# Causal softmax attention on one core: transposes of the weights three tiles behind the scores instead of two

## The chip, the cores and the metric

One of the cores of a Trainium2 chip runs the whole program. The metric is the device time in microseconds (us) of one execution. The core's engines used here are TensorE (PE, with PEld for its weight loads), VectorE (DVE), ScalarE (ACT), GpSimd (POOL) and the queue of SyncE (SP), which issues the DMAs. Each engine works through its own instructions in order; they wait for each other by semaphores.

## The reference

The program is a transformer-like chain with residual additions: attention A, a feed-forward layer, attention B (hyperbolic distances), and the feed-forward layer again. The change lies in attention A alone, with 2 batches of 2048 tokens, 16 heads of width 64:

```
x = x + attn_a(layernorm(x));  x = x + ffn(layernorm(x));  x = x + attn_b(layernorm(x));  x = x + ffn(layernorm(x))
attn_a:
    q, k, v = x @ Wq, x @ Wk, x @ Wv                      # 16 heads of 64
    scores = q @ k.T * 64**-0.5 + slope[h] * (i - j)      # masked where j > i
    out = softmax(scores) @ v                             # all heads side by side
    return out @ Wo + bo
```

All data are float32.

## The kernel before

Attention A works through 2 batches, and in each through 8 pairs of heads. A loop over the batches holds a loop of 7 turns over the first seven pairs, and after it the eighth pair written out once more. So of the 16 pairs 12 are followed by a taken branch back to the start of the loop's body, 2 by the branch that isn't taken, and 2 end a batch. Before the pairs of a batch all four engines make the normalized and transposed input `xnT` and the projections q and k of the first pair.

A query tile is 128 rows. The 16 tiles of a pair are taken from the longest (tile 15, all 2048 key columns) to the shortest (tile 0, 128 columns, since the mask is causal). The work on the n-th of them is:

- **S(n)**, "scores": TensorE multiplies q by k for both heads at once into PSUM, in slots of up to 512 columns (4 slots for n = 0 to 3, then 3, 2 and 1). VectorE adds the position bias, writes the row to `srow` in SBUF and takes the row's maximum in the same instruction (L598), one for each head and slot. Two slots have PSUM banks, so that TensorE is at most two slots ahead of VectorE (L758). L604 makes the negated maximum of the tile.
- **exponential** (ScalarE, L674): one for each head over the whole row, in place, with the sum. ScalarE issues both for tile n-1 at the start of step n, ahead of its copies of that step.
- **invert** (VectorE, L579 and L582): reciprocal of the sum and multiplication of the row, for tile n-1 in step n, one head in the middle of the step and one at its end.
- **T**, "transposes": TensorE transposes the weights out of `srow` in groups of four blocks of 128 x 128, each head to itself, into a ring of three PSUM banks (L773). The first group of a tile waits for `scaled`, that is for L582 (L770). ScalarE and VectorE copy each bank to `pT` (L523 and L661). A fixed table, `on_dve`, says which of the two engines does it, and each entry waits until the entry three before it has been copied (L490).
- **A(k)**, "product with v": for two tiles at once, once both are transposed (L791). **C(k)**: ScalarE copies the result to `oT`. **O(k)**: TensorE multiplies by Wo (L802) and VectorE adds to X (L615).
- **V**: four groups of projections of v (L743), in steps 0 and 1. **P**: the eight projections of q and k for the next pair (L730), in the last four steps, two in each. VectorE copies k, ScalarE copies q.

The order is written by `order(n)`: for each step n a list of these items, which every engine follows for its own part. In a step S, A and T are interleaved slot by slot. Before the change T of tile n-2 stands in step n, A and C in the even steps from 4, O in the odd ones from 5, and a pair has 20 steps. A row of `srow` may be overwritten once the tile that held it has been transposed (L593). After the last step VectorE branches back to the next pair's first step at L651, TensorE at L836 and ScalarE at L711.

Of the kernel before, what the change touches and what calls it, by code (L numbers as in the profile page):

```python
# [20 lines left out]
TB = SEQ // P  # L21
# [357 lines left out]
def stage_attn_a(nc, env, wqk, wv, wo, bo, slopes):  # L379
# [11 lines left out]
    parts = [[(a, min(a + 4, 2 * ib + 2)) for a in range(0, 2 * ib + 2, 4)] for ib in reversed(range(NIB))]  # L391
    part0 = [sum(len(c) for c in parts[:k]) for k in range(NIB + 1)]
    NPA = part0[NIB]
    ROWS = 3
    LAG = 2
    STEPS = TB + 4
    PROJ = ["q3", "k0", "k1", "k2", "k3", "q2", "q1", "q0"]
    NPR = len(PROJ)

    def order(n):  # L400

        m, k = n - LAG, (n - 4) // 2
        s = [("S", i) for i in range(len(slots[n]))] if n < TB else []
        t = [("T", i) for i in range(len(groups[m]))] if 0 <= m < TB else []
        a = [("A", i) for i in range(len(parts[k]))] if n >= 4 and n % 2 == 0 else []
        seq = []
        for i in range(max(len(s), len(t), len(a), 1)):
            seq += s[i:i + 1]  # L410
            if i == 0 and n >= 5 and n % 2:
                seq += [("O", k)]
            seq += a[i:i + 1] + t[i:i + 1]
            if n < 2 and i % 2:
                seq += [("V", 2 * n + i // 2)]
        if a:
            seq += [("C", k)]
        if n >= TB:
            seq += [("P", 2 * (n - TB)), ("P", 2 * (n - TB) + 1)]
        return seq  # L420


    ring = []
    for n in range(STEPS):
        for what, i in order(n):
            ring += {"T": [("T", n - LAG, i, 0), ("T", n - LAG, i, 1)], "V": [("V", i)], "O": [("O", i)]}.get(what, [])
    NEV = len(ring)
# [4 lines left out]
    def count(upto):  # L432
        return sum(on_dve[:upto])
# [4 lines left out]
    with ExitStack() as ctx:  # L438
        def sb(n, shape, dt=F32):
            return ctx.enter_context(nc.sbuf_tensor(f"a_{n}", shape, dt))  # L440
# [14 lines left out]
        v_sb = sb("v", [P, TB, 2 * DH])  # L455
        srow = sb("srow", [P, ROWS, 2, SEQ])
        xn = srow[:, 0, 0, 0:4 * D].rearrange("p (j d) -> p j d", d=D)
# [21 lines left out]
        def bank(i, a=0, b=BANK):  # L479
            return env.psum[:, i * BANK + a:i * BANK + b]  # L480

        def rows(h):
            return slice(h * DH, (h + 1) * DH)
# [25 lines left out]
        def copy_weights(eng, copy, g, n, i, dve_side):  # L509
            a, z = groups[n][i]  # L510
            il = tiles[n] % 2
            for h in range(2):
                e = place["T", n, i, h]
                if on_dve[e] != dve_side:
                    continue
                eng.wait_ge(bank_done, g * NEV + e + 1)

                if n >= 2:
                    k = n // 2 - 1
                    eng.wait_ge(av_done, g * NPA + (part0[k] + i + 1 if n % 2 == 0 else part0[k + 1]))  # L520
                else:
                    eng.wait_ge(av_done, g * NPA)
                copy(pT[:, h, a:z, il * P:(il + 1) * P],  # L523
                     bank(T_BANKS[e % 3], 0, (z - a) * P).rearrange("p (j i) -> p j i", i=P)
                     ).then_inc(dve_evac if dve_side else act_evac, 1)
# [37 lines left out]
        def _(dve):  # L563
# [9 lines left out]
            def body(b, hp, last):  # L573
# [3 lines left out]
                def invert(m, h):  # L577
                    dve.wait_ge(exp_done, (g * TB + m) * 2 + h + 1)
                    nc.vector.reciprocal(zinv[:, m, h:h + 1], zsum[:, m, h:h + 1]).then_inc(zinv_done, 1)  # L579
                    dve.wait_ge(zinv_done, (g * TB + m) * 2 + h + 1)  # L580
                    row = srow[:, m % ROWS, h, 0:(tiles[m] + 1) * P]
                    nc.vector.tensor_scalar(row, row, zinv[:, m, h:h + 1], None, ALU.mult).then_inc(scaled, 1)  # L582

                for n in range(STEPS):
                    m = n - 1
                    seq = order(n)
                    for j, (what, i) in enumerate(seq):
                        if what == "S":
                            a, z = slots[n][i]
                            c = slot0[n] + i  # L590
                            if i == 0:

                                dve.wait_ge(bank_done, g * NEV + (tile_end[n - ROWS] if n >= ROWS else 0))  # L593
                            off = SEQ - P - tiles[n] * P
                            for h in range(2):
                                dve.wait_ge(scores_done, (g * NSL + c) * 2 + h + 1)
                                dve.sem_inc(passed, 1)
                                nc.vector.tensor_tensor_reduce(  # L598
                                    out=srow[:, n % ROWS, h, a:z], in0=bank(c % 2 * 2 + h, 0, z - a),
                                    in1=bias[:, h, off + a:off + z], scale=1.0, scalar=-3e38, op0=ALU.add, op1=ALU.max,  # L600
# [7 lines left out]
                        if what == "T":  # L608
                            copy_weights(dve, nc.vector.tensor_copy, g, n - LAG, i, True)
                        if what == "O":  # L610
# [46 lines left out]
        def _(act):  # L657
# [12 lines left out]
            def exponential(g, n, h):  # L670
                width = (tiles[n] + 1) * P
                act.wait_ge(nmax_done, g * TB + n + 1)
                row = srow[:, n % ROWS, h, 0:width]
                nc.scalar.activation(row, row, ACT.Exp, bias=nmax[:, n, h:h + 1],  # L674
                                     accum_out=zsum[:, n, h:h + 1]).then_inc(exp_done, 1)

            def body(b, hp, last):
                g = b * PAIRS + hp
                for n in range(STEPS):
                    m = n - 1  # L680
# [3 lines left out]
                    for j, (what, i) in enumerate(seq):  # L684
# [4 lines left out]
                        if what == "T":  # L689
                            copy_weights(act, copy, g, n - LAG, i, False)  # L690
                        if what == "C":
# [24 lines left out]
        def _(pe):  # L716
# [17 lines left out]
            def values(g, i):  # L734

                if i == 0:
                    pe.wait_ge(wv_loaded, (g + 1) * 16)
                e = place["V", i]
                bank_free(pe, g, e)
                ps = bank(T_BANKS[e % 3])  # L740
                for t in range(4):
                    for c in range(KC):
                        last = nc.tensor.matmul(ps[:, t * P:(t + 1) * P], xnT[:, c, (4 * i + t) * P:(4 * i + t + 1) * P],  # L743
                                                wv_sb[:, c, :], start=(c == 0), stop=(c == KC - 1))
                last.then_inc(bank_done, 1)

            def scores(g, n, i):
                a, z = slots[n][i]
                c = slot0[n] + i
                if c == 0:  # L750

                    pe.wait_ge(k_copied, (g + 1) * 4)
                    pe.wait_ge(q_copied, g * 4 + 2)
                if c == 1:
                    pe.wait_ge(q_copied, (g + 1) * 4)
                if c >= 2:

                    pe.wait_ge(max_done, (g * NSL + c - 1) * 2)  # L758
                pe.sem_inc(passed, 1)
                for h in range(2):  # L760
                    nc.tensor.matmul(bank(c % 2 * 2 + h, 0, z - a), q_sb[rows(h), tiles[n] * P:(tiles[n] + 1) * P],  # L761
                                     k_sb[rows(h), a:z], start=True, stop=True, skip_group_check=True
                                     ).then_inc(scores_done, 1)

            def transposes(g, n, i):
                a, z = groups[n][i]
                for h in range(2):
# [4 lines left out]
                    for jt in range(a, z):  # L772
                        last = nc.tensor.transpose(bank(T_BANKS[e % 3], (jt - a) * P, (jt - a + 1) * P),  # L773
                                                   srow[:, n % ROWS, h, jt * P:(jt + 1) * P], env.ident[:, :])
                    last.then_inc(bank_done, 1)

            def product_with_v(g, k, i):


                ib = NIB - 1 - k  # L780
                if i == 0:

                    e = tile_end[2 * k + 1]
                    pe.wait_ge(dve_evac, g * n_dve + count(e))
                    pe.wait_ge(act_evac, g * n_act + e - count(e))
                    pe.wait_ge(oT_done, g * NIB + k)
                    pe.sem_inc(passed, 1)
                for jt in range(*parts[k][i]):
                    lo = P if jt == 2 * ib + 1 else 0
                    for h in range(2):  # L790
                        last = nc.tensor.matmul(bank(6, lo, IB)[rows(h), :], v_sb[:, jt, rows(h)], pT[:, h, jt, lo:IB],  # L791
                                                start=(jt == 0), stop=(jt == 2 * ib + 1), skip_group_check=True)
                last.then_inc(av_done, 1)
# [12 lines left out]
            def body(b, hp, last):  # L806
                g = b * PAIRS + hp
                for n in range(STEPS):
                    for what, i in order(n):
                        if what == "S":  # L810
                            scores(g, n, i)
                        if what == "V":
                            values(g, i)
                        if what == "T":
                            transposes(g, n - LAG, i)
                        if what == "A":
                            product_with_v(g, (n - 4) // 2, i)
                        if what == "O":
                            out_projection(g, i)
                        if what == "P" and not last:  # L820
                            project(g + 1, i)
# [808 lines left out]
```

## Time and profile before

| | before |
|---|---|
| median of 3 runs | 6132.58 us (6128.41 to 6133.12) |
| profiled execution, its own time | 6132.41 us |
| span of the profiled execution | 6130.6 us |
| attention A in it | from about 48 to 2339 us |
| one head pair inside the loop | 141.3 us (632.24 to 773.54 us) |
| PE busy | 4058.3 us (66% of the span) |
| DVE busy | 4679.5 us (76%) |
| ACT busy | 4508.2 us (74%) |
| POOL busy | 1421.4 us (23%) |

The span is the time from the first to the last instruction in the record of one execution. A busy time is the union of the instructions' durations on an engine, over all stages together. The stages have different limits, so that these shares don't say what bounds attention A; the rows of a pair do. In a timeline a row merges neighbouring instructions of one form, and a bracket at its end gives how long the engine had been idle before it and which instruction ended that wait.

### The profile page before, as it was taken

What the parts mean: (1) busy time and instruction counts of PE and PEld (TensorE: products, weight loads), DVE (VectorE), ACT (ScalarE), POOL (GpSimd) and SP (SyncE); (2) the same over time, 40 slices, a digit from 0 to 9 for tenths busy, and PEclk for the clock granted to TensorE, in tenths of its full rate; (3) what the DMA queues carried; (4) which work ended last, traced back from release to release, by engine and by line L of the source; (5) the groups of instructions that cost most, each with busy time, mean ns of one, the idle gap of its engine ahead of it and who ended that gap; (6) DMA issues with size and microseconds to landing.
All of it is one profiled execution on the core that took longest, in us unless ns stands there. A gap on an engine that the chain in (4) does not pass through costs nothing. (4 is left out here: it accounts for less than half of the span.)

```text
span 6130.6 us, 71245 instructions
## 1 busy us (share of the span) xinstructions
PE 4058.3 (66%) x22020; PEld 1846.5 (30%) x22020; DVE 4679.5 (76%) x7176; ACT 4508.2 (74%) x3663; POOL 1421.4 (23%) x1211
## 2 busy tenths in 40 slices
PE   6999999899999997444444444445355444444446
PEld 4555555555555555210101110102111111110104
DVE  6666666666666665699889898884889898989865
ACT  3555555455555553289999999996499999999992
POOL 0000000000000000144444444430244444445320
PEclk9999999999999997667767777777566677777767
DMA  1000000000000000288888888884488888888871
GB/s 35 5 5 5 5 8 5 5 6 5 5 5 5 5 2 3 77 173 184 182 186 182 185 185 181 186 172 120 123 186 183 180 187 180 188 174 185 181 153 58
DMA packets 137220, 628.82 MB, mean 103 GB/s; under 512 B 28038, under 2 KB 66120, under 8 KB 66632
## 3 DMA queue, kind: packets, MB, share of 16 engines
q0 software_dynamic: 73728, 536.90, 43.7%
q1 hardware_dynamic: 63048, 86.55, 4.1%
q8 instruction: 211, 3.46, 0.2%
q14 instruction: 233, 1.91, 0.1%
HBM read 65.30 MB, written 21.23 MB: 14 GB/s over the span
## 5 line engine op out<-in xcount | busy, mean ns | idle before, releaser
L1272 DVE SCALAR_TENSOR_TENSOR b_tiles<-b_ra_rep,b_cap,psum 128x1024 f32<-128x1024 f32 x1024 | 1260.7, 1270 | 246.9 <-PE psum L1503 234.7
L598 DVE CUSTOM_DVE_ANT_0 a_srow<-psum,a_bias 128x512 f32<-128x512 f32 (+3 forms) x1280 | 727.5, 607 | 518.0 <-PE psum L761 488.9
L1503 PE MATMUL psum<-b_qT,b_kT 126*128 126x512 bf16 x2048 | 763.4, 484 | 500.3 <-DVE b_tiles L1272 497.4
L661 ACT ACTIVATE a_pT<-psum 128x512 f32<-128x512 f32 (+3 forms) x1056 | 511.4, 527 | 656.1 <-PE psum L773 656.1
L1516 PE MATMUL psum<-b_tiles,b_v_aug 128*32 128x512 f32 x2464 | 449.3, 814 | 682.1 <-ACT b_tiles L1416 682.0
L1279 DVE TENSOR_SCALAR b_tiles<-b_tiles 128x2048 f32<-128x2048 f32 x512 | 665.6, 1300 | 5.5
L773 PE MATMUL psum<-ident,a_srow 128*128 128x128 f32 x4352 | 624.9, 280 | 67.7 <-DVE a_pT L523 31.1
L761 PE MATMUL psum<-a_k,a_q 64*128 64x512 f32 (+3 forms) x2560 | 626.8, 573 | 7.2 <-DVE a_cmax L598 6.1
L674 ACT ACTIVATE a_srow<-a_srow,a_nmax 128x1536 f32<-128x1536 f32 (+15 forms) x512 | 610.3, 1197 | 21.7 <-DVE a_nmax L604 19.6
L1416 ACT ACTIVATE b_tiles<-b_tiles,b_sc 128x4096 f32<-128x4096 f32 x154 | 585.5, 3802 | 5.1
L1516 PE MATMUL psum<-X,b_v_aug 128*32 128x512 f32 x1632 | 294.7, 806 | 442.2 <-ACT X L1416 442.2
L1403 ACT ACTIVATE b_tiles<-b_tiles 128x4096 f32<-128x4096 f32 x154 | 552.7, 3612 | 26.2 <-DVE b_tiles L980 25.3
L773 PEld LDWEIGHTS psum<-ident,a_srow 128*128 128x128 f32 x4352 | 474.8, 140 | 317.7 <-issue 146.4
L199 POOL MEMSET ffn_rank<- 128x1 f32 x16 | 0.7, 99 | 2413.4 <-POOLq L74 2413.4
L1410 ACT ACTIVATE b_tiles<-b_tiles 128x4096 f32<-128x4096 f32 x154 | 555.8, 3609 | 0.9
L791 PE MATMUL psum<-a_pT,a_v 128*64 128x256 f32 (+1 forms) x4608 | 540.6, 374 | 15.1 <-ACT a_pT L661 11.6
L980 DVE TENSOR_TENSOR b_tiles<-b_tiles 128x2048 f32<-128x2048 f32 x232 | 535.8, 2310 | 0.6
L1503 PEld LDWEIGHTS psum<-b_qT,b_kT 126*128 126x128 bf16 x2048 | 156.8, 108 | 1237.3 <-DVE b_tiles L1272 945.3
L980 POOL TENSOR_TENSOR b_tiles<-b_tiles 128x2048 f32<-128x2048 f32 x76 | 273.4, 3597 | 651.9 <-PE psum L1516 643.4
L582 DVE TENSOR_SCALAR a_srow<-a_srow,a_zinv 128x1536 f32<-128x1536 f32 (+15 forms) x512 | 402.8, 787 | 18.2
L791 PEld LDWEIGHTS psum<-a_pT,a_v 128*64 128x64 f32 x4608 | 312.2, 136 | 283.5 <-issue 171.8
L1403 ACT ACTIVATE X<-X 128x4096 f32<-128x4096 f32 x102 | 366.7, 3612 | 39.1 <-DVE X L980 38.5
(209 smaller groups left out, 5887.2 us busy)
## 6 DMA issues: line engine op xcount, KB each, us to landing
b_tiles<-b_tiles POOLq DMA_DIRECT2D x308, 1024.0 KB, 12.7
X<-b_tiles POOLq DMA_DIRECT2D x204, 1024.0 KB, 12.9
b_ra_rep<-ra_scratch SPq DMA_DIRECT2D x32, 1024.0 KB, 6.8
x_scratch<-X SPq DMA_DIRECT2D x8, 1024.0 KB, 10.6
kv_scratch<-b_tiles SPq DMA_DIRECT2D x4, 2048.0 KB, 8.6
X<-x_scratch SPq DMA_DIRECT2D x8, 1024.0 KB, 10.7
X<-in_x_dram SPq DMA_DIRECT2D x4, 1024.0 KB, 9.4
a_wqk<-in_wqk_dram SPq DMA_DIRECT2D x32, 128.0 KB, 2.6
```

Of the source, the lines that this page charges most:

```text
L598: nc.vector.tensor_tensor_reduce(out=srow[:, n % ROWS, h, a:z], in0=bank(c % 2 * 2 + h, 0, z - a), in1=bias[:, h, off + a:off + z], scale= ...
L674: nc.scalar.activation(row, row, ACT.Exp, bias=nmax[:, n, h:h + 1], accum_out=zsum[:, n, h:h + 1]).then_inc(exp_done, 1)
L761: nc.tensor.matmul(bank(c % 2 * 2 + h, 0, z - a), q_sb[rows(h), tiles[n] * P:(tiles[n] + 1) * P], k_sb[rows(h), a:z], start=True, stop=Tru ...
L773: last = nc.tensor.transpose(bank(T_BANKS[e % 3], (jt - a) * P, (jt - a + 1) * P), srow[:, n % ROWS, h, jt * P:(jt + 1) * P], env.ident[:, :])
L791: last = nc.tensor.matmul(bank(6, lo, IB)[rows(h), :], v_sb[:, jt, rows(h)], pT[:, h, jt, lo:IB], start=(jt == 0), stop=(jt == 2 * ib + 1) ...
L980: engine.tensor_tensor(y_slot(h, k), a, a, ALU.mult).then_inc(S["sq_" + name], 1)
L1272: nc.vector.scalar_tensor_tensor(out=a[:, s * HALF:(s + 1) * HALF], in0=ra_rep[:, j, s * HALF:(s + 1) * HALF], scalar=cap[:, j, k:k + 1], ...
L1279: nc.vector.tensor_scalar(a, a, 1.0, 1.0 + GUARD, ALU.add, ALU.max).then_inc(S["a_ready"], 1)
L1403: nc.scalar.activation(y, y, ACT.Sqrt, bias=-1.0).then_inc(S["root_done"], 1)
L1416: nc.scalar.activation(y, y, ACT.Exp, bias=col(SHIFT), scale=col(NEG_S)).then_inc(S["w_done"], 1)
L1503: last = nc.tensor.matmul(half_ps(s)[:, i * BANK:(i + 1) * BANK], kT[:, j, k * P:(k + 1) * P], qT[:, j, cs], start=True, stop=True)
L1516: last = nc.tensor.matmul(bank(4 + j)[32 * i:32 * i + 32, :], v_aug[:, j, k, :], y_slot(h, k)[:, i * BANK:(i + 1) * BANK], start=(k == 0), ...
```

## The change

The transposes of a tile come three steps after its scores instead of two. Since a row then stays in use one step longer, `srow` gets four rows instead of three. Everything behind the transposes is one step later too: A and C stand in the odd steps from 5 to 19, O in the even ones from 6 to 20, and a pair has 21 steps. The projections for the next pair stay in steps 16 to 19, so that the last step holds O(7) alone. The order of the entries in the ring of PSUM banks, and which engine copies each, is the same as before, entry for entry.

```diff
-    ROWS = 3
-    LAG = 2
-    STEPS = TB + 4
+    ROWS = 4
+    LAG = 3
+    STEPS = TB + LAG + 2
...
-        m, k = n - LAG, (n - 4) // 2
+        m, k = n - LAG, (n - LAG - 2) // 2
         s = [("S", i) for i in range(len(slots[n]))] if n < TB else []
         t = [("T", i) for i in range(len(groups[m]))] if 0 <= m < TB else []
-        a = [("A", i) for i in range(len(parts[k]))] if n >= 4 and n % 2 == 0 else []
+        a = [("A", i) for i in range(len(parts[k]))] if n >= LAG + 2 and (n - LAG) % 2 == 0 else []
...
-            if i == 0 and n >= 5 and n % 2:
+            if i == 0 and n >= LAG + 3 and (n - LAG) % 2:
                 seq += [("O", k)]
...
-        if n >= TB:
+        if TB <= n < TB + 4:
             seq += [("P", 2 * (n - TB)), ("P", 2 * (n - TB) + 1)]
...
                         if what == "A":
-                            product_with_v(g, (n - 4) // 2, i)
+                            product_with_v(g, (n - LAG - 2) // 2, i)
```

TensorE, at the end of a pair inside the loop. L730 are projections for the next pair, L802 is O(7), L798 and L488 its waits for the copy of the result and for a free bank, and L836 is the branch back. The rows with a minus are of before, those with a plus of the change:

```order
-L798 REGISTER_ALU
-L488 REGISTER_ALU
-L802 MATMUL psum<-a_wo,a_oT 128x256 x2
 L728 REGISTER_ALU
 L730 MATMUL psum<-a_xnT,a_wqk 128x512 x2
 L728 REGISTER_ALU
 L730 MATMUL psum<-a_xnT,a_wqk 128x512 x2
+L798 REGISTER_ALU
+L488 REGISTER_ALU
+L802 MATMUL psum<-a_wo,a_oT 128x256 x2
 L836 REGISTER_ALU
 L836 COMPARE_AND_BRANCH
```

O(7) has moved from ahead of the last two projections, P6 and P7, to behind them, and is now the last thing that TensorE does in a pair.

TensorE, from the end of step 1 of a pair into step 2, before. L743 is the last group of v, L758 the wait for a free pair of score banks, L770 and L490 the waits of the transposes L773:

```order
L743 MATMUL psum<-a_wv,a_xnT 128x128 x8
L758 ISA
L761 MATMUL psum<-a_k,a_q 128x512 x2
L770 ISA
L490 REGISTER_ALU
L773 MATMUL psum<-ident,a_srow 128x128 x4
L770 REGISTER_ALU
```

The same engine with the change, from the third slot of step 2 to the first transposes, which now stand in step 3:

```order
L758 ISA
L761 MATMUL psum<-a_k,a_q 128x512 x2
L758 ISA
L761 MATMUL psum<-a_k,a_q 128x256 x2
L758 ISA
L761 MATMUL psum<-a_k,a_q 128x512 x2
L770 ISA
L490 REGISTER_ALU
L773 MATMUL psum<-ident,a_srow 128x128 x4
```

The four slots of step 2 now follow each other on TensorE with nothing between them, and the transposes of the first tile begin behind the first slot of step 3.

## Rows read from the trace of the kernel before

**Rows 1.** Windows inside one pair: step 2, step 3, and the pair's sum

```profile
648.57:657.89 9.32, 8.26 (x49) 4.59 (x48) 7.98 (x22) 7.33 (x11) 0.00 (x0) 1.00 0.05 15
657.89:666.23 8.34, 7.69 (x47) 4.39 (x46) 7.41 (x21) 6.65 (x11) 0.00 (x0) 1.00 0.01 3
...
sum 141.30, PE 135.36 PEld 80.26 DVE 93.46 ACT 76.93 POOL 0.00; mean PE 33.84 PEld 20.07 DVE 23.37 ACT 19.23 POOL 0.00
```

Their columns: from and to, length, then busy time and instructions of PE, PEld, DVE, ACT and POOL, granted clock, DMA share and GB/s; the sum has the busy times alone.

**Rows 2.** Groups by line of PE, over the same pair: busy, mean, idle before

```profile
L773 PE MATMUL psum<-ident,a_srow 128*128 128x128 f32 x272 | 39.1, 280 | 4.3 <-DVE a_pT L523 1.9 <-ACT a_pT L661 1.1 <-DVE a_srow L582 0.9
```

**Rows 3.** Timeline of PE at the loop's turn: start, length, instruction

```profile
627.85 1.03 PE L802 MATMUL psum<-a_wo,a_oT 128*128 128x256 f32 x4
628.72 3.60 PE L730 MATMUL psum<-a_xnT,a_wqk 128*128 128x512 f32 x8
632.24 1.99 PE L761 MATMUL psum<-a_k,a_q 64*128 64x512 f32 x8
634.16 2.05 PE L743 MATMUL psum<-a_wv,a_xnT 128*128 128x128 f32 x16
636.73 0.70 PE L761 MATMUL psum<-a_k,a_q 64*128 64x512 f32 x2 [0.51 <-DVE a_cmax L598]
```

**Rows 4.** Timeline of DVE at the same turn

```profile
629.03 0.69 DVE L615 TENSOR_TENSOR X<-psum,X 128x512 f32 x1 [2.00 <-PE psum L802]
635.27 0.69 DVE L598 CUSTOM_DVE_ANT_0 a_srow<-psum,a_bias 128x512 f32<-128x512 f32 x1 [5.55 <-PE psum L761]
```

**Rows 5.** Timeline of DVE where the branch isn't taken, after the seventh pair

```profile
1052.76 0.69 DVE L615 TENSOR_TENSOR X<-psum,X 128x512 f32 x1 [2.00 <-PE psum L802]
1057.30 0.69 DVE L598 CUSTOM_DVE_ANT_0 a_srow<-psum,a_bias 128x512 f32<-128x512 f32 x1 [3.84 <-PE psum L761]
```

**Rows 6.** Line L836, the branch of TensorE: least, median and greatest duration in ns

```profile
L836 PEldq COMPARE_BRANCH  x14: 83/3749/5093, 201.5 to 2201.7; - x14
```

**Rows 7.** Timeline of DVE in steps 2 and 3 of the pair

```profile
650.00 0.68 DVE L598 CUSTOM_DVE_ANT_0 a_srow<-psum,a_bias 128x512 f32<-128x512 f32 x1
...
650.61 0.69 DVE L598 CUSTOM_DVE_ANT_0 a_srow<-psum,a_bias 128x512 f32<-128x512 f32 x1
...
653.53 1.22 DVE L582 TENSOR_SCALAR a_srow<-a_srow,a_zinv 128x1920 f32<-128x1920 f32 x1
...
657.12 0.42 DVE L598 CUSTOM_DVE_ANT_0 a_srow<-psum,a_bias 128x256 f32<-128x256 f32 x1 [0.35 <-PE psum L761]
```

**Rows 8.** Timeline of ACT in steps 2 and 3 of the pair

```profile
651.05 1.89 ACT L674 ACTIVATE a_srow<-a_srow,a_nmax 128x1920 f32<-128x1920 f32 x1
...
652.93 1.07 ACT L661 ACTIVATE a_pT<-psum 128x512 f32<-128x512 f32 x2
...
658.13 1.79 ACT L674 ACTIVATE a_srow<-a_srow,a_nmax 128x1792 f32<-128x1792 f32 x1
```

**Rows 9.** Timeline of PE in steps 2 and 3 of the pair

```profile
653.57 0.66 PE L773 MATMUL psum<-ident,a_srow 128*128 128x128 f32 x4 [1.06 <-ACT a_pT L661]
...
660.26 0.65 PE L773 MATMUL psum<-ident,a_srow 128*128 128x128 f32 x4 [0.65 <-DVE a_srow L582]
```

**Rows 10.** Timeline of PE in steps 9 to 17 of the pair before

```profile
581.57 0.33 PE L773 MATMUL psum<-ident,a_srow 128*128 128x128 f32 x1 [1.06 <-DVE a_pT L523]
...
608.87 0.87 PE L791 MATMUL psum<-a_pT,a_v 128*64 128x256 f32 x8
...
610.31 1.13 PE L802 MATMUL psum<-a_wo,a_oT 128*128 128x256 f32 x4
...
612.82 1.74 PE L791 MATMUL psum<-a_pT,a_v 128*64 128x256 f32 x16 [0.72 <-ACT a_pT L661]
...
619.83 0.33 PE L773 MATMUL psum<-ident,a_srow 128*128 128x128 f32 x1 [0.28 <-DVE a_srow L582]
```

**Rows 11.** Timeline of PE between the batches

```profile
1190.38 1.97 PE L829 MATMUL psum<-ident,a_srow 128*128 128x128 f32 x8 [4.91 <-DVE a_srow L635]
```

**Rows 12.** A window behind it, with the columns of rows 1

```profile
1204.00:1209.60 5.60, 5.52 (x7) 2.43 (x8) 0.66 (x1) 0.60 (x1) 0.00 (x0) 0.50 0.00 0
```

## The prediction

> **What bounds the kernel now.** I read three things, each to answer one question. First, what limits attention A? The windows over one pair of heads inside the loop [rows 1] show TensorE busy for 135.4 of 141.3 us at full clock, VectorE for 93.5 and ScalarE for 76.9. So attention A is TensorE's work, one piece after another, plus 5.9 us a pair in which it stands still. The change gives TensorE no work more and none less: only those 5.9 us can shrink or grow, in 16 pairs. Second, what makes TensorE stand still? The group of the transposes [rows 2] has 4.3 us of it, and only 0.9 of them end with L582, the scaled row. The other 3.0 end with a copy that frees a bank of the ring, and the change leaves the ring as it is. Third, where does TensorE have little beside the scores? In steps 2 and 3 it still stands still for 1.06 and 0.65 us [rows 1], with VectorE busy for 8.0 and 7.4 us, and at the loop's turn, where the other engines start again. There I followed the timelines.
>
> **The turn of the loop.** O(7) ends on TensorE at 628.88 (627.85 + 1.03). While VectorE adds its result and branches back, TensorE has P6 and P7 (3.6 us), then slots 0 and 1 of the next pair (1.9) and the first group of v (2.05), and stands still only 0.51 us before slot 2 at 636.73 [rows 3]. Slot 2 needs VectorE to have read slot 0. VectorE adds at 629.03 and reads slot 0 only at 635.27, 6.24 us later [rows 4]. Those scores were not what it waited for: slot 0 starts at 632.24. After the seventh pair, where the branch isn't taken, the same distance is 4.54 us and ends about as the scores get there [rows 5]. The taken branch therefore keeps VectorE away until some 6.2 us after the add begins. Slot 2 starts 636.73 - 628.88 = 7.85 us after O(7)'s end whatever TensorE does in between. The Trainium skill states this ("Runtime: NRT & Kernel Launch", the section on instruction fetch mechanics): a taken branch to a page outside the current window has to wait for a DMA fetch of that page. It gives no time for it, and the sum uses none.
>
> With the change O(7) is behind P6 and P7. It still has the two projections between itself and A(7), so that its own wait stays covered, and VectorE's branch still begins only after O(7). What is left to TensorE in the 7.85 us is slots 0 and 1 and one group of v: 634.16 - 632.24 + 2.05 = 3.97 us. It stands still for 3.88 instead of 0.51: **+3.37 us, 12 times = +40**. TensorE's own branch lies in it as well. Its record lasts up to 5.1 us and 3.7 in the middle [rows 6]; before, it ran under the queued projections, and now it can begin only once O(7) is released, about 0.6 us after A(7)'s end (the copy to `oT`), with 4.5 us of work still queued. That may delay slot 0 by about a us, but slot 2 waits for VectorE anyway. At the four pair ends without a taken branch nothing is added.
>
> **The start of a pair.** Step 2 loses its transposes, 32 of 0.144 us (39.1 / 272 [rows 2]) = 4.6 us, and keeps four slots. Then VectorE sets the rate, since TensorE is at most two slots ahead. VectorE begins slot 0 of step 2 at 650.00, one head each 0.61 us, and an inversion 1.22 with some 0.15 ahead of it for the reciprocal [rows 7]. With nothing else in the way: slot 0 until 651.2, slot 1 until 652.45, first inversion until 653.8, slot 2 until 655.05, slot 3 (256 columns, 0.35 a head) until 655.75, maximum at 656.0, second inversion until 657.4. TensorE has slots 0 and 1 done by 650.7, starts slot 2 at 651.4 (0.7 idle), slot 3 behind it until 653.2, and waits until 655.2 for slot 2's maximum, before slot 0 of step 3 (2.0 idle). That is 2.8 us in the step.
>
> Step 3 then has T(0). Its first banks are copied by ScalarE behind both exponentials of tile 2. Before, in step 2, the second of them ran from 651.05 and the copies followed at 652.93 [rows 8], and TensorE waited 1.06 us for it [rows 9]. Now the exponentials start at the maximum, 656.05, take 2 x 1.79, and the first copy is done at 660.3. TensorE wants the bank at 659.0: slot 0 from 655.2, four transposes twice, slot 1, and one head's group. Idle 1.35 us. The same pattern in step 4 leaves about 0.3. Against that, the 1.06 of step 2 and the 0.65 of step 3, which ended with the scaled row [rows 9], are gone. 2.8 + 1.35 + 0.3 - 1.06 - 0.65 = **+2.74 us a pair, x 16 = +44**. A bound from below is 0, if the pattern of step 3 only moves; from above some 4, if step 4 has a wait like step 3's.
>
> **What is gained later.** The wait of 1.06 us for a copy on VectorE in step 9 [rows 10], and one like it of 0.86 in step 13, come because that copy stands behind S of the same step and one inversion. S and the inversion are one tile shorter there with the change, so that the copy comes about 0.6 and 0.3 us earlier. **-0.9 x 16 = -14.** In the last steps A(6) waited 0.72 us for the copies of T(13); P0 and P1 now stand between them. The last transposes waited 0.28 us for the scaled row, and are now a step behind it. O(5), though, has lost the slot of S(15) that stood between it and A(5): A(5) ended at 609.74 (608.87 + 0.87) and O(5) started at 610.31 behind that slot. TensorE now waits those 0.57 us, where it waited 0.14 before. -0.72 - 0.28 + 0.43 = -0.57, in the 14 pairs that have P: **-8**. VectorE's and ScalarE's own load is the same, and SP's loads wait for the same events; nothing of the other stages moves.
>
> **Sum:** 40 + 44 - 14 - 8 = +62 on the profiled execution's 6132.4, which is 0.2 below the median: **6194 us**, +1.0%. Faster or slower by 0.2% (12 us) is about what a measurement tells from no change.
>
> **The rivals.**
>
> *Faster.* The lag was the trouble, and everything TensorE waits for in a pair after its first two steps goes: the 4.3 us at the transposes [rows 2] and the 0.72 before A(6), x 16 = -80, while the start costs nothing because VectorE's backlog in step 2 is made up in step 3; the turn keeps its +40. That gives 6092. It decides in step 2: it needs VectorE to read four slots while TensorE loses less than 1 us there. Against it are the 8.0 us of VectorE in that step beside 3.9 of TensorE's, and that three quarters of the waits aren't for the scaled row. With a part of this, and no cost at the start, the time is within 12 us of before. Chances 0.07 and 0.06.
>
> *The turn costs nothing.* If VectorE's absence at the turn begins with something other than O(7), its restart would come earlier as well. Then +22 is left: 6154. That the 6.24 us follow the add in all 12 turns speaks against it. 0.08.
>
> *The clock falls at the turn.* Between the batches TensorE stands still for 4.91 us [rows 11], and in the window behind it the granted clock is 0.5, 1.2 GHz, and still is in the first 5.6 us of dense projections [rows 12]. Gaps up to 1.1 us inside a pair left it at 2.4 GHz. The new gap of 3.9 us lies between. A fall could cost half of 5.6 us of dense work, 2.8, at each of 12 turns: +34, 6228. If TensorE's branch delays slot 0, the gap is in two parts, of 1 and 2.9 us, which speaks against it. The Trainium skill ("TensorE: Matmul & The Clock Gate") has a rule of thumb that idle gaps over about 3 us bring the slow level back; it would put this rival first, and the time at 6228. No gap of 3.9 us is in the trace. 0.14.
>
> *Forecast,* waits at start and turn at full clock: 0.65, with a range of its own from 6167 to 6214 (start from 0 to 4 us, less what the later steps give, the turn from 3 to 4).
>
> **Numbers.** From 6148 to 6230 holds the forecast, the costless turn and most of the clock rival. Slower 0.87, within 0.2% 0.06, faster 0.07.
>
> **What would show it.** In the changed profile TensorE's gap before slot 2 of a pair (released by VectorE's L598) should be 3 to 4 us in 12 pairs and near 0 in those after an untaken branch; a pair in the loop should last about 145.5 to 146 us and a pair before an untaken branch about 3.4 less. In step 2 TensorE should wait twice for L598, 0.7 and 2.0 us, where L598 had almost no waiters; the wait for L582 should be gone, and the wait for ScalarE's copy should be in step 3. A granted clock below 1.0 inside a batch would show the clock rival. I'd be wrong if VectorE's restart doesn't follow O(7), or if TensorE makes up in the middle of a pair what it lost at its start; since it has no slack there, it can't by these rows.

## The result and the profile after

The changed kernel takes 6229.57 us (median of 4 runs, 6224.62 to 6231.33) against 6132.85 before (4 runs): 1.6% slower, ratio 1.0158 (1.014 to 1.0176). That is inside the range, but only 0.4 us under its top. The forecast of the likeliest case was 6194, 36 us less. The number is near the 6228 of the rival in which the clock falls too, but only in part for that rival's reasons. The profiled execution took 6224.62 us with a span of 6222.7, 92.1 more than before.

TensorE's busy time on the page rose from 4058.3 to 4081.5 us with the same number of instructions, and the granted clock has new dips inside attention A. The rest is idle time. The groups of TensorE over attention A show what it waited for (count, busy and mean, idle before it and what ended it). Two of them before, and then the changed kernel's:

```profile
L761 PE MATMUL psum<-a_k,a_q 64*128 64x512 f32 (+3 forms) x2560 | 626.8, 573 | 7.2 <-DVE a_cmax L598 6.1
L743 PE MATMUL psum<-a_wv,a_xnT 128*128 128x128 f32 x1024 | 131.3, 281 | 0.0
```

```profile
L761 PE MATMUL psum<-a_k,a_q 64*128 64x512 f32 (+3 forms) x2560 | 640.9, 587 | 88.3 <-DVE a_cmax L598 71.8 <-issue 14.1
L773 PE MATMUL psum<-ident,a_srow 128*128 128x128 f32 x4352 | 623.2, 282 | 52.2 <-DVE a_pT L523 26.2 <-ACT a_pT L661 12.9 <-DVE X L615 10.2
L791 PE MATMUL psum<-a_pT,a_v 128*64 128x256 f32 (+1 forms) x4608 | 540.6, 374 | 5.6 <-DVE a_pT L523 2.1 <-ACT a_pT L661 1.5 <-issue 0.2
L802 PE MATMUL psum<-a_wo,a_oT 128*128 128x256 f32 x512 | 142.5, 401 | 17.3 <-ACT a_oT L661 17.3
L743 PE MATMUL psum<-a_wv,a_xnT 128*128 128x128 f32 x1024 | 137.7, 290 | 0.0
```

| TensorE stands still before | before, us | after, us | difference | forecast |
|---|---|---|---|---|
| scores, L761 | 7.2 | 88.3 | +81 | 12 x 3.37 + 16 x 2.8 = +85 |
| transposes, L773 | 67.7 | 52.2 | -16 | -1 - 14 - 4 = -19 |
| product with v, L791 | 15.1 | 5.6 | -10 | -10 |
| output projection, L802 | 7.1 | 17.3 | +10 | +6 |
| all four | 97 | 163 | **+66** | **+62** |

The waits came nearly as forecast, and the scaled row (L582) no longer ends any. Of the scores' 88.3 us, 42.3 stand at the 12 turns with a taken branch (the waits before slots 0 and 2 added up), where 6.1 stood before: +36 against a forecast of +40. What the forecast left out is the other part: 66 + 23 of busy time is 89 of the 92 us of span. The busy time grew where the scores (+14.1) and v (+6.4) stand, the two kinds of work behind a turn.

The turn after the fourth pair, TensorE and then VectorE, in answer to [rows 3, 4]:

```profile
656.36 1.03 PE L802 MATMUL psum<-a_wo,a_oT 128*128 128x256 f32 x4
657.50 1.99 PE L761 MATMUL psum<-a_k,a_q 64*128 64x512 f32 x8
659.42 2.05 PE L743 MATMUL psum<-a_wv,a_xnT 128*128 128x128 f32 x16
665.00 3.79 PE L761 MATMUL psum<-a_k,a_q 64*128 64x512 f32 x8 [3.53 <-DVE a_cmax L598]
```

```profile
657.53 0.69 DVE L615 TENSOR_TENSOR X<-psum,X 128x512 f32 x1 [6.43 <-PE psum L802]
663.55 0.69 DVE L598 CUSTOM_DVE_ANT_0 a_srow<-psum,a_bias 128x512 f32<-128x512 f32 x1 [5.32 <-issue]
```

O(7) is now followed at once by the next pair. VectorE reads slot 0 6.02 us after it begins O(7)'s addition (6.24 before), and the profile names no instruction that it waited for. Slots 2 and 3 then take 3.79 us, where slots 0 and 1 took 1.99, and where slots 2 and 3 took 2.35 at this place before. The windows over this pair (columns as in [rows 1]) show why, and where the rest went:

```profile
657.50:668.72 11.22, 7.69 (x33) 3.84 (x33) 4.53 (x13) 0.60 (x1) 0.00 (x0) 0.77 0.16 40
668.72:679.04 10.32, 10.32 (x66) 7.71 (x64) 7.67 (x24) 5.04 (x6) 0.00 (x0) 0.92 0.01 2
679.04:685.69 6.65, 3.82 (x17) 1.38 (x17) 6.58 (x18) 4.35 (x5) 0.00 (x0) 1.00 0.06 20
685.69:694.96 9.27, 8.11 (x50) 4.81 (x52) 8.45 (x28) 6.83 (x11) 0.00 (x0) 1.00 0.01 2
...
sum 149.05, PE 137.35 PEld 81.64 DVE 94.19 ACT 76.86 POOL 0.00; mean PE 27.47 PEld 16.33 DVE 18.84 ACT 15.37 POOL 0.00
```

The pair lasts 149.05 us, 7.75 more than before; the forecast was 145.5 to 146. In the first window the mean granted clock is 0.77; from 665.00 to 668.72, the time of slots 2 and 3, it is 0.50, the level of 1.2 GHz:

```profile
665.00:668.72 3.72, 3.72 (x9) 1.20 (x9) 2.39 (x8) 0.00 (x0) 0.00 (x0) 0.50 0.00 0
```

Such a stretch follows 10 of the 12 turns with a taken branch. In the kernel before there is none inside a pair. Of the windows over the pair the third row is step 2: 3.82 us of TensorE's work in 6.65 us, with VectorE busy for 6.58 of them. TensorE's timeline there, in answer to [rows 9]:

```profile
681.92 1.92 PE L761 MATMUL psum<-a_k,a_q 64*128 64x512 f32 x8 [0.89 <-DVE a_cmax L598]
685.69 1.13 PE L761 MATMUL psum<-a_k,a_q 64*128 64x512 f32 x4 [1.85 <-DVE a_cmax L598]
...
690.65 0.66 PE L773 MATMUL psum<-ident,a_srow 128*128 128x128 f32 x4 [1.16 <-ACT a_pT L661]
...
698.90 0.65 PE L773 MATMUL psum<-ident,a_srow 128*128 128x128 f32 x4 [0.34 <-ACT a_pT L661]
```

0.89 and 1.85 stand against a forecast of 0.7 and 2.0, 1.16 in step 3 against 1.35, 0.34 in step 4 against 0.3.

The later steps of the pair before, in answer to [rows 10]:

```profile
608.36 0.33 PE L773 MATMUL psum<-ident,a_srow 128*128 128x128 f32 x1 [0.84 <-DVE a_pT L523]
...
620.40 0.88 PE L773 MATMUL psum<-ident,a_srow 128*128 128x128 f32 x6 [0.64 <-DVE X L615]
...
628.38 1.13 PE L802 MATMUL psum<-a_wo,a_oT 128*128 128x256 f32 x4 [0.33 <-ACT a_oT L661]
...
631.54 0.33 PE L773 MATMUL psum<-ident,a_srow 128*128 128x128 f32 x1 [0.80 <-DVE a_pT L523]
...
636.66 1.13 PE L802 MATMUL psum<-a_wo,a_oT 128*128 128x256 f32 x4 [0.56 <-ACT a_oT L661]
```

The waits of 1.06 and 0.86 are 0.84 and 0.80 now. Two are new. In step 12 the last transposes wait for O(3)'s addition (0.64): step 11 before, the one with T(9), had a slot of scores between its two groups of transposes, and step 12 has only one slot. In step 14 O(4) has a shorter slot ahead of it (0.33).

### The profile page after: what moved, and what is told of

Read it like the earlier page. It is cut to its first block and busy times, and to the rows that moved or that the text cites. A ratio compares the mean times of both kernels' runs of the same rounds, so it can differ in the third digit from the quotient of the medians.

```text
span 6222.7 us, 71229 instructions
## 1 busy us (share of the span) xinstructions
PE 4081.5 (66%) x22020; PEld 1864.8 (30%) x22020; DVE 4685.9 (75%) x7176; ACT 4507.7 (72%) x3663; POOL 1419.5 (23%) x1211
## 5 line engine op out<-in xcount | busy, mean ns | idle before, releaser
L598 DVE CUSTOM_DVE_ANT_0 a_srow<-psum,a_bias 128x512 f32<-128x512 f32 (+3 forms) x1280 | 727.1, 608 | 482.4 <-PE psum L761 410.7
L761 PE MATMUL psum<-a_k,a_q 64*128 64x512 f32 (+3 forms) x2560 | 640.9, 587 | 88.3 <-DVE a_cmax L598 71.8
L773 PE MATMUL psum<-ident,a_srow 128*128 128x128 f32 x4352 | 623.2, 282 | 52.2 <-DVE a_pT L523 26.2
L674 ACT ACTIVATE a_srow<-a_srow,a_nmax 128x1536 f32<-128x1536 f32 (+15 forms) x512 | 609.6, 1196 | 47.5 <-DVE a_nmax L604 47.5
L773 PEld LDWEIGHTS psum<-ident,a_srow 128*128 128x128 f32 x4352 | 482.1, 142 | 292.8 <-issue 139.6
L791 PE MATMUL psum<-a_pT,a_v 128*64 128x256 f32 (+1 forms) x4608 | 540.6, 374 | 5.6 <-DVE a_pT L523 2.1
L582 DVE TENSOR_SCALAR a_srow<-a_srow,a_zinv 128x1536 f32<-128x1536 f32 (+15 forms) x512 | 402.9, 787 | 18.1
L1416 ACT ACTIVATE X<-X,b_sc 128x4096 f32<-128x4096 f32 x102 | 387.8, 3802 | 3.4
```

The costliest lines, as they stand in the source:

```text
L598: nc.vector.tensor_tensor_reduce(out=srow[:, n % ROWS, h, a:z], in0=bank(c % 2 * 2 + h, 0, z - a), in1=bias[:, h, off + a:off + z], scale= ...
L1416: nc.scalar.activation(y, y, ACT.Exp, bias=col(SHIFT), scale=col(NEG_S)).then_inc(S["w_done"], 1)
```

## The experiments

Each edit is on the kernel before or on the changed one, and each ratio is to the kernel before on the same chip, whose medians there lie from 6131.2 to 6133.6 us. So differences between two kernels timed on different chips are uncertain by some 2 us.

**The cover alone given back.** Changed kernel:

```diff
-        if TB <= n < TB + 4:
-            seq += [("P", 2 * (n - TB)), ("P", 2 * (n - TB) + 1)]
+        if TB + 1 <= n < TB + 5:
+            seq += [("P", 2 * (n - TB - 1)), ("P", 2 * (n - TB - 1) + 1)]
```

> The changed kernel (lag of three, four rows, 21 steps) with the projections P for the next pair one step later, in steps 17 to 20, so that O(7) again has P6 and P7 behind it at the loop's turn. If the turn's cost is the lost cover (my theory), TensorE's wait before slot 2 of a pair falls from 3.5 us to about 0.5 at 12 turns (-40), the low clock behind it goes (about -14), and A(6), which waits for the copies of T(13) again, gives back about 8: some 6183 us, with the wait of 2.8 us in step 2 still there. If the turn costs nothing and the loss is the start of the pair alone, the time stays near 6229. If lag and rows as such are what costs, as before.

Measured: 6182.31 us, ratio 1.008 (1.0063 to 1.0096). As expected, 47 of the 97 us are gone by putting the projections behind O(7). The start of the pair is as in the changed kernel. A(6) waits again: the idle time before the product with v is 15.8 us, where the changed kernel has 5.6. So the turn itself costs some 57 us (47 + 10) without its cover.

**The cover alone taken away.** Kernel before, in the last step only:

```diff
-            if i == 0 and n >= 5 and n % 2:
+            if i == 0 and n >= 5 and n % 2 and n < STEPS - 1:
                 seq += [("O", k)]
...
             seq += [("P", 2 * (n - TB)), ("P", 2 * (n - TB) + 1)]
+        if n == STEPS - 1:
+            seq += [("O", k)]
```

> The kernel before (lag of two, three rows, 20 steps) with one edit: in the last step O(7) stands behind P6 and P7 instead of ahead of them. My theory: VectorE's branch starts after O(7), so TensorE loses its cover of 3.4 us at 12 turns, +40, and some of the low clock windows seen with the change appear too, +10 to +15: 6173 to 6188 us. If the turn is not tied to O(7), within 6 us of 6133.

Measured: 6195.59 us, ratio 1.0102 (1.0085 to 1.0119), +64: two thirds of the change's loss, with lag and rows as before. TensorE's timeline at a turn (this kernel's L763 is L761, its L600 is L598) and the windows around it:

```profile
648.88 1.99 PE L763 MATMUL psum<-a_k,a_q 64*128 64x512 f32 x8
650.80 2.05 PE L745 MATMUL psum<-a_wv,a_xnT 128*128 128x128 f32 x16
657.00 3.79 PE L763 MATMUL psum<-a_k,a_q 64*128 64x512 f32 x8 [4.15 <-DVE a_cmax L600]
```

```profile
648.00:662.00 14.00, 9.85 (x43) 5.55 (x42) 5.60 (x16) 1.19 (x2) 0.00 (x0) 0.76 0.13 31
```

Over attention A the scores' idle time went from 7.2 to 47.5 us, +40.3 (the term of the sum was 40), and that of the transposes and of the product stayed (67.8 and 15.2). The remaining 24 us, 2.0 a turn, came with the low clock, which here stands behind all 12 turns: the scores are busy for 643.7 us (626.8 before) and the projections of v for 138.6 (131.3), 24 more together. That is above the 10 to 15 I expected for it.

**The wait filled.** Changed kernel, behind the first group of v in all pairs but the last of a batch:

```diff
                             values(g, i)
+                            if i == 0 and not last:
+                                for _ in range(4):
+                                    nc.tensor.matmul(bank(6), wv_sb[:, 0, :], xnT[:, 0, 0:BANK], start=True, stop=True,
+                                                     skip_group_check=True)
```

> The changed kernel with four unused matmuls of 128x128 by 512 columns (3.4 us at full clock, into the bank of the products, which nobody reads at that point) behind the first group of v in every pair but the eighth of a batch. They fill TensorE's wait for slot 2. If the low clock behind that wait costs time, the windows at half clock near slot 2 go and the time falls by 10 to 20 us, less 2 x 3.4 at the two pairs that begin a batch and have no such wait: 6216 to 6226. If the low clock there costs nothing, it rises to about 6236 by those two pairs.

Measured: 6219.15 us, ratio 1.0142 (1.0125 to 1.0159): 10.4 us faster than the changed kernel (9.3 if each is taken against the kernel before that was timed beside it) with 112 more matmul records on TensorE, and in the range expected for a low clock that costs time. At a turn:

```profile
659.24 3.60 PE L816 MATMUL psum<-a_xnT,a_wv 128*128 128x512 f32 x8
663.15 2.35 PE L761 MATMUL psum<-a_k,a_q 64*128 64x512 f32 x8 [0.31 <-DVE a_cmax L598]
```

Slots 2 and 3 take 2.35 us instead of 3.79, and no low clock follows any turn. So the low clock behind the wait has a price of its own. The 10.4 us are not exactly that price: at the two pairs without a wait the unused work costs up to 3.4 us each, and the stretches of low clock behind step 2, ten in the changed kernel, are down to four. At a turn the unused work costs nothing, since slot 2 waits for VectorE anyway. This is a measurement of the clock's part, and no improvement to keep: giving back the cover saves the wait as well.

**Rows alone.** Kernel before with `ROWS = 4`.

> The kernel before with four score rows instead of three and nothing else (lag of two, 20 steps). A fourth row removes only a wait of VectorE for the transposes of the tile three back, which the trace before doesn't show as binding: within 5 us of 6133. If the rows themselves cost or gain (another layout in SBUF), it differs by more.

Measured: 6130.47 us, ratio 0.9998 (0.9988 to 1.0008). As expected, the rows cost and bring nothing.

**The projections of v spread over three steps.** The first experiment's kernel, and:

```diff
-            if n < 2 and i % 2:
-                seq += [("V", 2 * n + i // 2)]
+            if n < 2 and i == 1:
+                seq += [("V", n)]
+            if n == 2 and i in (0, 3):
+                seq += [("V", 2 + i // 3)]
```

> The changed kernel with P one step later, and besides it the four groups of v spread: one in step 0, one in step 1, two in step 2, where TensorE has lost the transposes. If TensorE's 2.8 us in step 2 are an accident of where v stands, about 2.5 us a pair come back (-40, 6142). My theory is that VectorE sets the end of step 2 over the first three steps together (8 + 8 + 8 heads of a slot and four inversions), so that filling step 2 only moves the wait to earlier steps, and at most the 1.5 us that VectorE waits in step 1 come back: 6158 to 6175 against 6182.

Measured: 6178.01 us, ratio 1.0072 (1.0055 to 1.0089). That is above the 6158 to 6175 I expected: 4 us below the first experiment, or 6 if each is taken against the kernel before on its own chip, and the intervals of the two ratios overlap. Steps 0 to 3 of one pair, here:

```profile
499.42:506.51 7.09, 6.23 (x34) 3.20 (x33) 3.99 (x13) 1.20 (x2) 0.00 (x0) 1.00 0.18 42
506.51:513.54 7.03, 5.94 (x32) 3.21 (x33) 6.59 (x20) 4.56 (x5) 0.00 (x0) 1.00 0.00 0
513.54:521.96 8.42, 7.64 (x48) 5.06 (x48) 7.61 (x22) 4.35 (x5) 0.00 (x0) 1.00 0.01 2
521.96:530.98 9.02, 7.92 (x50) 4.62 (x49) 8.27 (x27) 7.24 (x11) 0.00 (x0) 1.00 0.07 18
```

Together 31.56 us, where the first experiment's kernel has 32.37 for the same four. TensorE's idle time moved from step 2 (now 0.8 us) to steps 0 and 1 (0.9 and 1.1). VectorE is busy for 6.6, 7.6 and 8.3 us of steps 1 to 3, which last 7.0, 8.4 and 9.0. By these rows it sets the pace at the start of a pair, wherever v stands. No low clock is left behind step 2 here, so that part of the small gain may be the clock's.

**A projection ahead of A(6), first try.** Kernel before:

```diff
-        if n >= TB:
-            seq += [("P", 2 * (n - TB)), ("P", 2 * (n - TB) + 1)]
+        seq += [("P", i) for i in {TB - 1: [0], TB: [1, 2], TB + 1: [3], TB + 2: [4, 5], TB + 3: [6, 7]}.get(n, [])]
```

> The kernel before (lag of two, three rows) with the projections P in steps 15 to 19 as 1, 2, 1, 2, 2 instead of two each in 16 to 19: P0 now stands between T(13) and A(6), which waited 0.72 us for the copies of T(13); O(7) still has P6 and P7 behind it. If that wait is covered, 14 x 0.7 = 10 us less than before: 6122. If it moves (to P0's wait for the last maximum, or to O(6)), 6128 to 6133.

Measured: 6140.74 us, ratio 1.001 (1.0001 to 1.002), above both values expected. A(6)'s wait is gone, but the single projection behind T(15) doesn't cover the copy that A(7) needs. That copy is VectorE's, behind the 2.5 us of the next pair's bias (here L790 is L791, L522 is L523):

```profile
616.43 1.73 PE L790 MATMUL psum<-a_pT,a_v 128*64 128x256 f32 x16
...
626.80 0.87 PE L790 MATMUL psum<-a_pT,a_v 128*64 128x256 f32 x8 [1.31 <-DVE a_pT L522]
```

**The same spread with the lag of three,** steps 16 to 20: `{TB: [0], TB + 1: [1, 2], TB + 2: [3], TB + 3: [4, 5], TB + 4: [6, 7]}`.

> The changed kernel (lag of three) with P in steps 16 to 20 as 1, 2, 1, 2, 2: P6 and P7 stand behind O(7) and P0 between T(13) and A(6). Cover at the turn as in the first experiment (6182), and the 0.76 us before A(6) gone as in the changed kernel: about 6172. If the lag of three were worth something once both are covered, it would be below 6132.

Measured: 6171.94 us, ratio 1.006 (1.0043 to 1.0077). As expected. With the turn and A(6) covered, the lag of three still stands 38 us above the kernel before, and 48 above the lag of two with A(6) covered (second try, below).

**The start filled.** The first experiment's kernel with two unused matmuls behind the last slot of step 2:

```diff
                             scores(g, n, i)
+                            if n == 2 and i == 3:
+                                for _ in range(2):
+                                    nc.tensor.matmul(bank(6), env.ident[:, :], xnT[:, 0, 0:BANK], start=True, stop=True,
+                                                     skip_group_check=True)
```

> The first experiment's kernel (changed, P one step later) with two unused matmuls of 512 columns (1.7 us) behind the last slot of step 2, where TensorE waits 2 us for VectorE. If the windows of low clock behind step 2 (in 10 of 16 pairs) cost time, they go and the time falls by about 10 us, to 6172. If they cost nothing, it stays within 4 us of 6182.

Measured: 6179.61 us, ratio 1.0074 (1.0057 to 1.009): 2.7 us less than the first experiment, or 4.5 if each is taken against the kernel before on its own chip, where I expected 10 if the low clock cost time and at most 4 if it didn't. The intervals of the two ratios overlap, so no cost is shown. (By the trace of the first experiment's kernel a low window follows step 2 in 11 of the 16 pairs, one more than I had counted, and here in none.) Step 3 in the first experiment's kernel, and in this one:

```profile
523.16:532.49 9.33, 9.33 (x49) 5.52 (x49) 8.28 (x26) 6.64 (x10) 0.00 (x0) 0.82 0.01 2
```

```profile
522.29:531.37 9.08, 7.92 (x50) 4.62 (x49) 8.33 (x27) 6.64 (x10) 0.00 (x0) 1.00 0.01 2
```

At 0.82 of the clock TensorE is busy for all 9.33 us; at full clock it is busy for 7.92 and waits for ScalarE's copy in the rest. The step lasts 0.25 us less. A low clock is cheap where the engine would have waited next.

**No taken branch.** Changed kernel with the inner loop written out, on VectorE (the part shown), ScalarE and TensorE:

```diff
-                with dve.Fori(0, PAIRS - 1) as hp:
+                for hp in range(PAIRS - 1):
                     body(b, hp, False)
```

> The changed kernel with the inner loop over the head pairs written out on VectorE, ScalarE and TensorE, so that no branch is taken between the pairs of a batch; the same instructions in the same order otherwise. My theory: VectorE's taken branch is what TensorE waits for at slot 2 of a pair, so the 12 waits of some 3.5 us and the low clock behind them go: about 6229 - 59 = 6171 us, near the version with P behind O(7) and a P ahead of A(6). If the wait came from O(7)'s result or from the scores, and not from the branch, the time stays near 6229. If fetching straight-line code stalls the engines as well, something in between.

Measured: 6156.52 us, ratio 1.004 (1.0026 to 1.0054): 73 us less, with the order of the instructions untouched, and 14 more than I expected. VectorE behind O(7):

```profile
638.64 0.69 DVE L615 TENSOR_TENSOR X<-psum,X 128x512 f32 x1 [6.32 <-PE psum L802]
639.85 0.69 DVE L598 CUSTOM_DVE_ANT_0 a_srow<-psum,a_bias 128x512 f32<-128x512 f32 x1 [0.52 <-PE psum L761]
```

1.2 us instead of 6.0, and it is the scores that end the wait. What happens at a taken branch can be seen in the DMA queues that bring instructions. The kernel before, in the 8 us behind the addition of O(7) at the turn of [rows 4] (from 629 to 637 us: packets, MB, share):

```profile
q14 instruction: 5, 0.04, 1.8%
q8 instruction: 1, 0.02, 0.8%
```

All 12 turns with a taken branch have these five and one, and the two where the branch isn't taken have none. So instructions are fetched while VectorE is away. That its wait is for this fetch isn't shown by itself, but the profile names no instruction that ends it.

**The same on the kernel before.**

> The kernel before with the inner loop over the pairs written out in the same way. Its turn costs TensorE 0.5 us at 12 places: about 6132 - 6 = 6126 us. If fetching straight-line code stalls, more than 6133.

Measured: 6119.44 us, ratio 0.9981 (0.9971 to 0.9991), -12, twice what I expected. Each turn cost 1.0 us (a pair in the loop lasts 141.3 us, here 140.3), of which the visible gap before slot 2 is only 0.51. Slots 2 and 3 at the turn, in the loop and here:

```profile
636.73 2.35 PE L761 MATMUL psum<-a_k,a_q 64*128 64x512 f32 x8 [0.51 <-DVE a_cmax L598]
```

```profile
634.16 1.99 PE L761 MATMUL psum<-a_k,a_q 64*128 64x512 f32 x8
```

Another 0.36 us is the slower passage of these two slots, in the loop held up by VectorE a second time before slot 3.

**A projection ahead of A(6), second try.** Kernel before with P as `{TB - 1: [0], TB: [1], TB + 1: [2, 3], TB + 2: [4, 5], TB + 3: [6, 7]}`.

> The kernel before with the projections P in steps 15 to 19 as 1, 1, 2, 2, 2. P0 stands between T(13) and A(6) as in the earlier attempt with 1, 2, 1, 2, 2, where the wait came back as 1.3 us before a product with v; here T(15) keeps two projections between itself and A(7). If that was the place, 14 x 0.7 = 10 us less than before: 6122.

Measured: 6121.46 us, ratio 0.9983 (0.9973 to 0.9992), -10, as expected. The idle time before the product with v fell from 15.1 to 4.8 us.

**Both.**

> Both of these edits on the kernel before: inner loop written out, P as 1, 1, 2, 2, 2. If they add up, 6132 - 6 - 10 = 6116 us, below both kernels.

Measured: 6108.87 us, ratio 0.9962 (0.9948 to 0.9976). At -22 us the two gains, 12 and 10, add up; the expectation of 6116 had the loop's at 6. This kernel is 0.4% faster than the kernel before, and 1.9% faster than the changed one.

## Why the prediction was right, and where it was short

- **What bounds attention A** held: TensorE's work stayed the same, and every us lost or gained stands in its idle time or its clock.
- **The turn** was right in mechanism and in the size of its wait: 40.3 us where O(7) alone was moved, and 36 in the changed kernel, against 12 x 3.37 = 40. That it is the taken branch is shown by the loop written out. Changed less before, with and without the loop, gives the turn's net cost: (6229.6 - 6156.5) - (6131.2 - 6119.4) = 61 us. The term was short by some 20, because it priced a wait at full clock. They lie in the low clock behind the wait, and in what else a restart costs; filling the wait brought back 10.4 us, after what the unused work costs at the pairs without a wait.
- **The start of a pair** was right in its waits (0.89 + 1.85 = 2.74 in step 2 against 2.8; steps 3 and 4 within 0.2). With the loop written out in both, the lag costs 6156.5 - 6119.4 = 37 us for everything but the turn, against 44 - 14 - 8 = 22. In the prediction's working, 0.7 + 2.0 is 2.7 and not 2.8; step 2 has 0.09 us more before slot 3, which makes 2.83.
- **What is gained later** is the term that was mis-sized. Of the -0.9 a pair in steps 9 and 13 only 0.3 came, and the waits of step 12 (0.64) and of O(4) (0.33) weren't foreseen: the slot of scores that stood between two groups, or ahead of O, is shorter or missing once S is a tile further on. I had counted that for O(5) and not for its neighbours. (The reason is read from the order of the items, and no run tests it by itself.) The covered waits of A(6) and of T(15) were right: L791 lost 9.5 of the 10 us.
- **The clock rival,** at 0.14 and 6228, was right that the clock falls at the turn, and the forecast of full clock there was wrong. That 6228 is so near to 6229.57 is luck: its price of 34 us was too high for a turn that missed its term by 21 in all, and the other 15 are the later steps' missing gain. That the time is just inside the range is luck too. The argument against it was that TensorE's branch could split the wait in two. It did in seven of the 12 turns (1.7 to 1.9 us before slot 0, 0.3 to 2.7 before slot 2), and two of the seven, after the tenth and the eleventh pair, kept the full clock; the other five didn't, and neither did the five turns with one long wait (3.2 to 4.1 us). After the sixth pair slots 0 and 1 ran at the low level already:

```profile
956.39 3.17 PE L761 MATMUL psum<-a_k,a_q 64*128 64x512 f32 x8 [1.90 <-issue]
959.49 2.50 PE L743 MATMUL psum<-a_wv,a_xnT 128*128 128x128 f32 x16
962.28 2.35 PE L761 MATMUL psum<-a_k,a_q 64*128 64x512 f32 x8 [0.28 <-DVE a_cmax L598]
```

  The rule of thumb of the Trainium skill ("TensorE: Matmul & The Clock Gate", "Why this matters for your kernels") that idle gaps over about 3 us bring back the slow level agrees with the gap of 3.53 us here. It doesn't cover the gap of 1.90 us in these rows, nor the low windows behind step 2, where TensorE's longest gap was 1.85 us.
- **The costless turn** is excluded by O(7) moved alone, which cost 64 us, and by the loop written out, and **faster** by the changed kernel with both covers, still 38 us slower than before.

At the start of a pair the terms add up: the forecast 22, 21 more for the later steps (2.86 us of waits in steps 5 to 14 where there were 2.44, against a forecast of 0.9 less), 4 less for steps 2 and 3, make 39 against 37 measured. The low windows behind step 2 add little to it. At the turn the 21 us beside the forecast wait are the low clock and the restart together, and how they divide stays open. The three measures of a turn without cover (64 us where O(7) alone was moved, 57 where the cover was given back, 61 from the loop written out) agree within 7 us. Of the 1.0 us that a turn costs even before, 0.51 + 0.36 is seen, and the rest stays open.

## What to carry to other kernels

Before moving an instruction to the end of a loop's body, look at what the engines do while the loop turns: the last work that releases the slowest restart (here VectorE's, 6 us) should have other work behind it on the bounding engine. A longer lag between producer and consumer takes work out of the first steps and puts it into the last ones. It pays only if the waits that it removes (here 0.9 us a pair for the scaled row) are more than what the emptied first steps lose to the engine that is next in line. And when a wait on TensorE grows to several us, price the low clock behind it too, at places where nothing else would have waited.

## What the runs showed that I had not expected

- Step 2 has 3.8 us of TensorE's work in 6.65, with gaps of 0.89 and 1.85 us, and in 11 of 16 pairs a stretch at 0.5 of the clock follows (first experiment). Two unused matmuls in the longer gap removed all of them.
- Writing out the loop of 7 pairs had no visible cost for fetching instructions: pairs of 140.3 us, all alike.
- TensorE's own branch delayed slot 0 of the next pair by 0 to 1.9 us with the change; VectorE was still the later of the two in all 12 turns, by 0.28 us at the least.
